# Scratch rows regrouped: fewer, larger DMAs for the attention stacks and the maxima

## The chip, the cores and the metric

The kernel runs on one core of a Trainium2 chip. The metric is the device time of one execution in microseconds (us). The engines that the text names are TensorE (PE in the profile, PEld for its weight loads), VectorE (DVE), ScalarE (ACT), GpSimd (POOL) and SyncE (SP), which here issues every DMA of the kernel.

## The reference

One block of a transformer on 16 batches of 256 tokens of 512 numbers. First a cross attention: 32 heads of 16 numbers, keys and values from a context of 256 tokens of 256 numbers, rotary positions on q and k, and a gated residual. Then a feed-forward part with a squared ReLU (512 to 2048 and back), an expert product weighted by the sum of the two largest routing logits, a layer norm and a second gated residual.

```python
q = apply_axial_rope((layernorm(x) @ Wq).reshape(b, n, 32, 16), pos)
k = apply_axial_rope(k, pos)            # k, v = split(ctx @ Wkv)
w = softmax(einsum('bqhd,bkhd->bhqk', q, k) / 4)
x = x + tanh(g_xattn) * (attn @ Wout + bout)
x = x + tanh(g_ffn) * (layernorm(shared(h) + moe(h)) * gamma + beta)   # h = layernorm(x)
```

## The kernel before

Every float32 product is made of three passes on TensorE: each operand is split into a rounded high part and a rest (`qT[0]`, `qT[1]` and so on, index 0 the high part), and the passes are high x high, rest x high, high x rest.

The program has an attention phase, one batch after the other, and a feed-forward phase. In the attention phase an iteration `i` has 16 steps; at each step TensorE makes the logits of two heads of two batches (`logits_a` for batch `i + 1`, three steps late, and `logits_b` for batch `i`), and the table `SCHEDULE` spreads the other jobs over the steps: turning q and k (`kT1` at step 9, `qT1` at step 12), the projections, the output product. `logits_a` is made only to find the maximum of each row: VectorE's `maxima` reduces it to `mneg`. `logits_b` is the transposed product, with the negative maxima as two further rows, and ScalarE takes its exponential.

A logit needs the contraction over 16 numbers of a head in three passes. They are made in one matmul: the operands are stacked in 48 partitions. In `st_q` the stack is (high, rest, high), in `st_k` (high, high, rest); two heads lie at partitions 0 and 64. The 16 slots of a stack are the 16 steps. Rows 48 and 49 of `st_q` hold the maxima (high part and rest), those of `st_k` ones.

The turned q and k lie in SBUF as 128 partitions, `(l q d)`, of 4 slots of 256 tokens: 4 groups of slots `l`, 2 heads `q`, 16 numbers `d`. `store_turned` writes both parts to a scratch tensor in DRAM (two DMAs of 512 KB, 128 rows of 4 KB). `load_stack` reads from it half a stack (8 slots): for each of the three places in the stack and each of the two heads one DMA of 16 rows and two pieces of 4 KB a row. `load_max` writes the maxima of 8 slots, turned by TensorE to `mT` (16 partitions of 256), into single partitions of `st_q`: for each part and each head one DMA of 8 rows of 1 KB.

SP issues all of this in one written order. An iteration of SP: second half of the stacks of batch `i + 1` (k, then q); x and residual tiles; maxima of the second half of batch `i`; more x and the context; store of k of batch `i + 2`; x1; first half of the k stack of `i + 2`; maxima of the first half of `i + 1`; store of q and first half of the q stack of `i + 2`; x1. A load waits for the store's semaphore before it is issued. TensorE waits for both stacks of a half before steps 3 and 11 (`st_in`) and for the maxima before `logits_b` of steps 0 and 8 (`m_in`).

Of the kernel before, what the change touches and what calls it, by code (L numbers as in the profile page):

```python
# [26 lines left out]
P = 128  # L27
# [20 lines left out]
INC = 16  # L48

Q_PARTS = (0, 1, 0)
K_PARTS = (0, 0, 1)
ROWS_A = 3 * HD
ROWS_B = ROWS_A + 2
STACK_DMAS = 2 * len(Q_PARTS) * 2
PASSES = ((0, 0), (1, 0), (0, 1))


# [83 lines left out]
def flamingo_gated(nc, x, ctxT, posT, g_x, g_f, wq, wkv, wout, bout, gate, up, down, wexp, gamma, beta, out):  # L143
# [1 line left out]
    out_d = out.rearrange("b (t p) d -> (b t) p d", p=P)  # L145
    ctx_d = ctxT.rearrange("b (c p) s -> b p c s", p=P)

    qk_d = [[nc.dram_tensor(f"{x}T_scratch{par}", [2, P, KC * S], F32, kind="Internal").ap() for x in "qk"]
            for par in range(2)]
    x1_d = nc.dram_tensor("x1_scratch", [NT, P, D], F32, kind="Internal").ap()  # L150

    with ExitStack() as stack:
# [67 lines left out]
        aT = [sb1(f"aT{i}", [P, KC, P], F32R) for i in range(2)]  # L220
        xres = [sb1(f"xres{i}", [P, D]) for i in range(2)]
        gbout = sb1("gbout", [P, D])
        mneg = [sb1(f"mneg{i}", [P, TT, NH]) for i in range(2)]
        mT = [sb1(f"mT{i}", [NH // 2, S], F32R) for i in range(2)]
        rot_q1 = sb1("rot_q1", [P, D])
        rot = {"Q0": rot_q0, "Q1": rot_q1, "K0": rot_k, "K1": rot_k}
# [197 lines left out]
        def _(sp):  # L424
# [13 lines left out]
            def store_turned(b, par, x):  # L438

                if some(b - 1):  # L440
                    for half in range(2):
                        sp.wait_ge(st_in[half], INC * STACK_DMAS * (b - 1))
                        alone(sp)
                dst, src = (qk_d[par][0], qT) if x == "q" else (qk_d[par][1], kT)
                sp.wait_ge(taken[BANK[x + "T1"]], number(x + "T1", b))
                alone(sp)
                for part in range(2):
                    sp.dma_start(dst[part], src[part][:].rearrange("p c s -> p (c s)").bitcast(F32)
                                 ).then_inc(turned_out[x], INC)

            def load_stack(b, par, half, x):
                if some((b - 2) * STEPS + 8 * (half + 1)):
                    sp.wait_ge(b_done, (b - 2) * STEPS + 8 * (half + 1))
                    alone(sp)
                slots = slice(8 * half, 8 * half + 8)
                dst, src, parts = ((st_q[par], qk_d[par][0], Q_PARTS) if x == "q" else
                                   (st_k[par], qk_d[par][1], K_PARTS))
                sp.wait_ge(turned_out[x], 2 * INC * (b + 1))
                alone(sp)
                for r, part in enumerate(parts):  # L460
                    heads = src[part].rearrange("(l q d) n -> q d l n", q=2, d=HD)
                    for q in range(2):
                        row = 64 * q + HD * r
                        sp.dma_start(dst[row:row + HD, slots, :].rearrange("d (l c) s -> d l (c s)", c=KC).bitcast(F32),  # L464
                                     heads[q, :, 2 * half:2 * half + 2, :]).then_inc(st_in[half], INC)

            def load_max(b, par, half):
                sp.wait_ge(taken[BANK[f"m{half}"]], number(f"m{half}", b))
                for part in range(2):
                    for q in range(2):  # L470
                        row = 64 * q + ROWS_A + part
                        sp.dma_start(st_q[par][row:row + 1, 8 * half:8 * half + 8, :].bitcast(F32),
                                     mT[part][q:NH // 2:2, :].bitcast(F32)).then_inc(m_in, INC)

            def store_x1(b, t):
                sp.wait_ge(taken[BANK[f"O{t}"]], number(f"O{t}", b))
# [241 lines left out]
        def _(act):  # L718
# [18 lines left out]
            def job(name, i, par):  # L737
                if not live(name, i) or (name not in TWO_STEP and name[0] != "V"):
                    return
                b, par, t = i + LAG[name], (par + LAG[name]) % 2, int(name[-1])  # L740
                bank = BANK[name]
                act.wait_ge(done[bank], number(name, b))
                psum = {"P": pP, "M": pM, "T": pT}[bank]
                turned_psum = psum[:, :].rearrange("p (c s) -> p c s", c=KC)
                cut = slice(t * P, (t + 1) * P)
                if name[0] == "V":
                    if some(b - 1):
                        act.wait_ge(av_done, GROUPS * (b - 1))
                    nc.scalar.copy(v_s[par][:, t, :, 0:HD],
                                   psum[:, :].rearrange("p (h e) -> p h e", h=NH)).then_inc(taken[bank], 1)  # L750
                elif name[0] == "m":
                    if some(2 * b + t):
                        act.wait_ge(m_in, 4 * INC * (2 * b + t))
                    nc.scalar.copy(mT[0][:], psum[0:NH // 2, 0:S]).then_inc(hi_made[bank], 1)
                elif name[0] == "X":
                    nc.scalar.copy(xnT[0][:], turned_psum).then_inc(hi_made[bank], 1)
                elif name[0] == "a":
                    nc.scalar.copy(aT[0][:], turned_psum).then_inc(hi_made[bank], 1)
                else:
                    if some(b):  # L760
                        act.wait_ge(turned_out[name[0]], 2 * INC * b)
                    if name[0] == "q":
                        nc.scalar.mul(qT[0][:, :, cut], turned_psum, SCALE).then_inc(hi_made[bank], 1)
                    else:
                        nc.scalar.copy(kT[0][:, :, cut], turned_psum).then_inc(hi_made[bank], 1)
# [96 lines left out]
        def _(pe):  # L862
# [21 lines left out]
            def job(name, i, par):  # L884
# [11 lines left out]
                if name[0] == "X":  # L896
                    pe.wait_ge(xn_made, TT * b + t + 1)
                    last = turn(psum, lambda c: xn[:, c * P:(c + 1) * P])
                elif name[0] == "Q":
                    last = product(psum[:, :], lambda a, c: xnT[a][:, c, :], lambda w, c: wq_s[w][:, c, :], KC, half)  # L900
                elif name[0] == "K":
                    pe.wait_ge(ctx_split, 2 * b + 2)
                    last = product(psum[:, :], lambda a, c: ctx_s[par][a][:, c, t * P:(t + 1) * P],
                                   lambda w, c: wk_s[w][:, c, :], CC, half)
                elif name[0] == "V":
                    last = product(psum[:, :], lambda a, c: ctx_s[par][a][:, c, t * P:(t + 1) * P],
                                   lambda w, c: wv_s[w][:, c, :], CC, half)
                elif name[0] == "O":
                    last = product(psum[:, :], lambda a, c: aT[a][:, c, :], lambda w, c: wo_s[w][:, c, :], KC, half)
                elif name[0] in "qk":  # L910
                    rope = name[0].upper() + name[-1]
                    pe.wait_ge(roped, len(ROPES) * b + ROPES.index(rope) + 1)
                    last = turn(psum, lambda c: rot[rope][:, c * P:(c + 1) * P])
                elif name[0] == "m":
                    pe.wait_ge(max_done, STEPS * b + 8 * (t + 1))
                    for u in range(TT):
                        last = nc.tensor.transpose(psum[0:NH // 2, u * P:(u + 1) * P],
                                                   mneg[par][:, u, t * 16:(t + 1) * 16], ident[:])
                elif name[:2] == "aT":
                    last = turn(psum, lambda c: attn[t][:, c * P:(c + 1) * P])  # L920
                else:
                    u = int(name[1])
                    pe.wait_ge(av_taken, GROUPS * b + GROUPS // 2 * (t + 1))
                    last = turn(psum, lambda c: av_s[:, GROUPS // 2 * t + c, u * P:(u + 1) * P])
# [14 lines left out]

            def logits_b(b, par, s):  # L940
                if s % 8 == 0:
                    pe.wait_ge(m_in, 4 * INC * (2 * b + s // 8 + 1))
                if some(STEPS * b + s):
                    pe.wait_ge(exp_done, STEPS * b + s)
                for t in range(TT):
                    for q in range(2):
                        rows = slice(64 * q, 64 * q + ROWS_B)
                        last = nc.tensor.matmul(pB[:, q, t * S:(t + 1) * S], st_k[par][rows, s, t * P:(t + 1) * P],  # L948
                                                st_q[par][rows, s, :], start=True, stop=True)
                last.then_inc(b_done, 1)  # L950
# [125 lines left out]
        def _(dve):  # L1076
# [159 lines left out]
            def maxima(b, par, u):  # L1236
                dve.wait_ge(a_done, STEPS * b + u + 1)
                nc.vector.tensor_reduce(  # L1238
                    mneg[par][:, :, 2 * u:2 * u + 2].rearrange("p t q -> p q t"),
                    pA[:, :, :].rearrange("p q (t k) -> p q t k", t=TT), AX.X, ALU.max,  # L1240
                    negate=True).then_inc(max_done, 1)

# [140 lines left out]
```

## Time and profile before

| | us |
|---|---|
| Median of 3 runs | 1703.81 |
| Lowest, highest | 1700.79, 1704.51 |
| The profiled execution | 1698.25 |
| Its span, first to last instruction | 1696.5 |
| PE busy in the span | 1580.5 (93%) |
| PEld busy | 1169.4 (69%) |
| DVE busy | 985.1 (58%) |
| ACT busy | 640.4 (38%) |
| POOL busy | 291.1 (17%) |

The mean granted clock of TensorE is 0.97 of full speed. The DMA queue of SP moved 152.93 MB, and its packets took 38.2% of the time of the 16 DMA engines over the span. "Busy" is the time in which an engine worked on at least one instruction; matmuls are pipelined, so a busy PE need not be at its peak. In the rows, L464 is the DMA of `load_stack`, L472 that of `load_max`, L448 that of `store_turned`, L478 that of `store_x1`, L936 the product of `logits_a`, L948 that of `logits_b`. A window's DMA share is the time that the packets starting in it took, over the 16 engines' time, so it can come out a little over 1; GB/s is what these packets moved.

### The profile page before, as it was taken

How to read it: one execution, taken by the hardware profiler on the slowest of the kernel's cores; microseconds unless marked ns; L12 is line 12 of the kernel's file. 1: busy time of each engine (PE TensorE's matmuls, PEld its weight loads, DVE VectorE, ACT ScalarE, POOL GpSimd, SP SyncE). 2: the span in 40 equal slices, each digit the busy share in tenths (PEclk: the TensorE clock that was granted, in tenths of full speed). 3: DMA queues.
4: the chain of work that ended last, by engine and by line, in shares of the span. 5: the costliest groups of instructions: out<-in, count | busy, mean ns of one | idle time of the engine just before them, and what ended most of it. 6: DMA issues, size and time to landing. Idle time of an engine off the chain costs nothing.

```text
span 1696.5 us, 27932 instructions
## 1 busy us (share of the span) xinstructions
PE 1580.5 (93%) x9760; PEld 1169.4 (69%) x9760; DVE 985.1 (58%) x1460; ACT 640.4 (38%) x960; POOL 291.1 (17%) x363
## 2 busy tenths in 40 slices
PE   3588999999999999988799999999999999999997
PEld 2355666666666666655477788887888878888786
DVE  4577787777778777865455443543435444263524
ACT  2135555555555555555343222221222222222221
POOL 3112222222222222101100110201102010020202
PEclk9679999999999999999799999999999999999999
DMA  3667666666777678773243010100101001010001
GB/s 118 143 145 157 171 141 157 155 147 159 161 144 161 136 158 169 150 144 84 69 124 94 23 35 19 50 26 26 32 19 50 25 26 37 13 50 25 32 19 38
DMA packets 76221, 153.99 MB, mean 91 GB/s; under 512 B 13296, under 2 KB 26608, under 8 KB 76144
## 3 DMA queue, kind: packets, MB, share of 16 engines
q1 hardware_dynamic: 76144, 152.93, 38.2%
q8 instruction: 53, 0.87, 0.2%
q14 instruction: 24, 0.20, 0.0%
HBM read 101.50 MB, written 50.33 MB: 89 GB/s over the span
## 4 chain that ended last, share of the span: by engine, by line
PE 72%; DMA 9%; DVE 8%; SPq 4%; issue 4%; ACT 1%; POOL 1%; DVEq 0%; POOLq 0%; ACTq 0%
PE pP L874 15%; PE pA L1033 10%; PE pO L874 10%; PE pB L1033 10%; PE pT L874 9%; PE pA L936 4%; PE pO L960 4%; DMA stq<-mT 3%; PE pM L874 3%; SPq L464 2%; DVE mneg L1238 2%; PE pB L948 2%; DMA qT_scratch<-qT 2%; PE pM L881 1%; DMA kT_scratch<-kT 1%
## 5 line engine op out<-in xcount | busy, mean ns | idle before, releaser
L1238 DVE TENSOR_REDUCE mneg<-pA 128x4 f32<-128x1024 f32 x256 | 313.1, 1223 | 170.9 <-PE pA L936 168.7
L797 ACT ACTIVATE probs<-pB 128x1024 f32<-128x1024 f32 x256 | 262.5, 1026 | 282.1 <-PE pB L948 274.4
L1308 DVE TENSOR_TENSOR relu<-relu 128x512 f32<-128x512 f32 x128 | 88.3, 690 | 266.6 <-ACT hid L832 266.6
L639 POOL TENSOR_SCALAR var_eps<-meanvar 128x1 f32<-128x1 f32 x96 | 34.5, 360 | 1093.0 <-DVE meanvar L1134 1093.0
L1033 PE MATMUL pA<-dn,hid 128*128 128x512 f32 x768 | 199.0, 394 | 2.8 <-DVE hid L1310 2.1
L1033 PE MATMUL pB<-dn,hid 128*128 128x512 f32 x768 | 196.1, 391 | 0.0
L874 PE MATMUL pO<-fT,up 128*128 128x512 f32 x768 | 188.9, 395 | 3.4 <-issue 3.4
L874 PE MATMUL pP<-fT,up 128*128 128x512 f32 x768 | 190.0, 396 | 0.0
L874 PEld LDWEIGHTS pO<-fT,up 128*128 128x128 f32 x768 | 145.2, 189 | 36.3 <-issue 4.2
L1033 PEld LDWEIGHTS pA<-dn,hid 128*128 128x128 f32 x768 | 142.9, 188 | 38.4 <-DVE hid L1310 7.1
L1033 PEld LDWEIGHTS pB<-dn,hid 128*128 128x128 f32 x768 | 144.2, 188 | 31.0
L936 PE MATMUL pA<-stk,stq 48*128 48x256 f32 x1024 | 133.3, 340 | 33.7 <-DVE mneg L1238 20.4
L874 PEld LDWEIGHTS pP<-fT,up 128*128 128x128 f32 x768 | 142.4, 188 | 30.9
L936 PEld LDWEIGHTS pA<-stk,stq 48*128 48x128 f32 x1024 | 79.5, 192 | 107.2 <-issue 63.5
L960 PE MATMUL pO<-probs,v 128*17 128x256 f32 x2048 | 140.2, 393 | 0.6 <-ACT probs L797 0.6
L825 ACT ACTIVATE relu<-pO 128x512 f32<-128x512 f32 x64 | 38.3, 599 | 254.8 <-PE pO L874 246.3
L948 PE MATMUL pB<-stq,stk 50*128 50x256 f32 x1024 | 106.8, 286 | 11.2 <-DMA stq<-mT 8.8
L825 ACT ACTIVATE relu<-pP 128x512 f32<-128x512 f32 x64 | 38.3, 599 | 197.9 <-PE pP L874 197.9
L874 PE MATMUL pP<-wq,xnT 128*128 128x512 f32 x384 | 108.7, 421 | 1.6 <-DVE xnT L1154 1.6
L874 PE MATMUL pT<-wo,aT 128*128 128x512 f32 x384 | 106.7, 423 | 2.8 <-DVE aT L1180 2.8
L874 PEld LDWEIGHTS pP<-wq,xnT 128*128 128x128 f32 x384 | 73.2, 200 | 29.7 <-issue 12.9
L874 PE MATMUL pT<-ex,fT 128*128 128x512 f32 x384 | 93.6, 392 | 0.0
(131 smaller groups left out, 1963.6 us busy)
## 6 DMA issues: line engine op xcount, KB each, us to landing
stk<-kT_scratch SPq DMA_DIRECT2D x192, 128.0 KB, 5.3
stq<-qT_scratch SPq DMA_DIRECT2D x192, 128.0 KB, 5.7
kT_scratch<-kT SPq DMA_DIRECT2D x32, 512.0 KB, 3.1
qT_scratch<-qT SPq DMA_DIRECT2D x32, 512.0 KB, 3.5
xin<-x SPq DMA_DIRECT2D x32, 256.0 KB, 7.3
xres<-x SPq DMA_DIRECT2D x32, 256.0 KB, 9.6
x_scratch<-xres SPq DMA_DIRECT2D x32, 256.0 KB, 3.7
fx<-x_scratch SPq DMA_DIRECT2D x32, 256.0 KB, 2.7
```

The source lines that it names most:

```text
L464: sp.dma_start(dst[row:row + HD, slots, :].rearrange("d (l c) s -> d l (c s)", c=KC).bitcast(F32), heads[q, :, 2 * half:2 * half + 2, :]). ...
L639: nc.gpsimd.tensor_scalar_add(var_eps[:], meanvar[:, 1:2], EPS).then_inc(ve_made, 1)
L797: nc.scalar.activation(probs[:, s % 4, :, :, :].rearrange("p a b s -> p a (b s)"), pB[:, :, :], ACT.Exp).then_inc(exp_done, 1)
L825: nc.scalar.activation(relu[m % 2][:], pU[m % 2], ACT.Relu).then_inc(relu_made, 1)
L874: last = nc.tensor.matmul(dst, lhs(a, c), rhs(w, c), start=(c == 0 and (a, w) == PASSES[0]), stop=(c == chunks_ - 1 and (a, w) == PASSES[-1]))
L881: last = nc.tensor.transpose(dst[:, c * P:(c + 1) * P], src(c), ident[:])
L936: last = nc.tensor.matmul(pA[:, q, t * S:(t + 1) * S], st_q[par][rows, s, t * P:(t + 1) * P], st_k[par][rows, s, :], start=True, stop=True)
L948: last = nc.tensor.matmul(pB[:, q, t * S:(t + 1) * S], st_k[par][rows, s, t * P:(t + 1) * P], st_q[par][rows, s, :], start=True, stop=True)
L960: last = nc.tensor.matmul(pO[32 * j:32 * j + HD + 1, 0:S], v_s[par][:, t, 4 * g + j, :], probs[:, (2 * g + j // 2) % 4, j % 2, t, :], star ...
L1033: last = nc.tensor.matmul(acc[u], hid[m % 2][x_][:, u * P:(u + 1) * P], dn_s[w][:, m, :], start=(m == 0 and k == 0), stop=(m == MC - 1 and ...
L1238: nc.vector.tensor_reduce(mneg[par][:, :, 2 * u:2 * u + 2].rearrange("p t q -> p q t"), pA[:, :, :].rearrange("p q (t k) -> p q t k", t=TT ...
L1308: nc.vector.tensor_tensor(r[:], r[:], r[:], ALU.mult).then_inc(sq_made, 1)
```

## The change

The scratch tensor of q and k is laid out as 2 parts of 32 rows (2 heads of 16 numbers) of all 16 slots, so that a row of a stack is one piece of 8 KB per half. The store writes the same 4 KB pieces to other places: its destination is `l r m`, 4 groups by 32 rows by 1024 numbers. `load_stack` takes two neighbouring places of the stack at once where their parts are 0 and 1 (q: places 0 and 1, then 2; k: place 0, then 1 and 2): four DMAs, two of 256 KB and two of 128 KB, not six of 128 KB. The columns of `mneg` are ordered by head and then slot, so that `mT` holds the 8 slots of one head and then those of the other, and `load_max` writes both heads' rows, partitions 48 and 112 or 49 and 113, with one DMA of 16 KB. The counts that wait for these DMAs follow.

```diff
--- before.py
+++ after.py
@@ -49,11 +49,11 @@
 
 
 
-Q_PARTS = (0, 1, 0)
-K_PARTS = (0, 0, 1)
+Q_RUNS = ((0, 0, 2), (2, 0, 1))
+K_RUNS = ((0, 0, 1), (1, 0, 2))
 ROWS_A = 3 * HD
 ROWS_B = ROWS_A + 2
-STACK_DMAS = 2 * len(Q_PARTS) * 2
+STACK_DMAS = 2 * len(Q_RUNS) * 2
 PASSES = ((0, 0), (1, 0), (0, 1))
 
 
@@ -145,7 +145,7 @@
     out_d = out.rearrange("b (t p) d -> (b t) p d", p=P)
     ctx_d = ctxT.rearrange("b (c p) s -> b p c s", p=P)
 
-    qk_d = [[nc.dram_tensor(f"{x}T_scratch{par}", [2, P, KC * S], F32, kind="Internal").ap() for x in "qk"]
+    qk_d = [[nc.dram_tensor(f"{x}T_scratch{par}", [2, 2 * HD, STEPS * S], F32, kind="Internal").ap() for x in "qk"]
             for par in range(2)]
     x1_d = nc.dram_tensor("x1_scratch", [NT, P, D], F32, kind="Internal").ap()
 
@@ -220,7 +220,7 @@
         aT = [sb1(f"aT{i}", [P, KC, P], F32R) for i in range(2)]
         xres = [sb1(f"xres{i}", [P, D]) for i in range(2)]
         gbout = sb1("gbout", [P, D])
-        mneg = [sb1(f"mneg{i}", [P, TT, NH]) for i in range(2)]
+        mneg = [sb1(f"mneg{i}", [P, TT, 2, 2, NH // 4]) for i in range(2)]
         mT = [sb1(f"mT{i}", [NH // 2, S], F32R) for i in range(2)]
         rot_q1 = sb1("rot_q1", [P, D])
         rot = {"Q0": rot_q0, "Q1": rot_q1, "K0": rot_k, "K1": rot_k}
@@ -445,7 +445,8 @@
                 sp.wait_ge(taken[BANK[x + "T1"]], number(x + "T1", b))
                 alone(sp)
                 for part in range(2):
-                    sp.dma_start(dst[part], src[part][:].rearrange("p c s -> p (c s)").bitcast(F32)
+                    sp.dma_start(dst[part].rearrange("r (l m) -> l r m", l=STEPS // KC),
+                                 src[part][:].rearrange("p c s -> p (c s)").bitcast(F32)
                                  ).then_inc(turned_out[x], INC)
 
             def load_stack(b, par, half, x):
@@ -453,24 +454,23 @@
                     sp.wait_ge(b_done, (b - 2) * STEPS + 8 * (half + 1))
                     alone(sp)
                 slots = slice(8 * half, 8 * half + 8)
-                dst, src, parts = ((st_q[par], qk_d[par][0], Q_PARTS) if x == "q" else
-                                   (st_k[par], qk_d[par][1], K_PARTS))
+                dst, src, runs = ((st_q[par], qk_d[par][0], Q_RUNS) if x == "q" else
+                                   (st_k[par], qk_d[par][1], K_RUNS))
                 sp.wait_ge(turned_out[x], 2 * INC * (b + 1))
                 alone(sp)
-                for r, part in enumerate(parts):
-                    heads = src[part].rearrange("(l q d) n -> q d l n", q=2, d=HD)
+                for r, part, n in runs:
                     for q in range(2):
                         row = 64 * q + HD * r
-                        sp.dma_start(dst[row:row + HD, slots, :].rearrange("d (l c) s -> d l (c s)", c=KC).bitcast(F32),
-                                     heads[q, :, 2 * half:2 * half + 2, :]).then_inc(st_in[half], INC)
+                        sp.dma_start(dst[row:row + n * HD, slots, :].rearrange("d l s -> d (l s)").bitcast(F32),
+                                     src[part:part + n, HD * q:HD * (q + 1), 8 * half * S:8 * (half + 1) * S]
+                                     ).then_inc(st_in[half], INC)
 
             def load_max(b, par, half):
                 sp.wait_ge(taken[BANK[f"m{half}"]], number(f"m{half}", b))
                 for part in range(2):
-                    for q in range(2):
-                        row = 64 * q + ROWS_A + part
-                        sp.dma_start(st_q[par][row:row + 1, 8 * half:8 * half + 8, :].bitcast(F32),
-                                     mT[part][q:NH // 2:2, :].bitcast(F32)).then_inc(m_in, INC)
+                    row = ROWS_A + part
+                    sp.dma_start(st_q[par][row:row + 65:64, 8 * half:8 * half + 8, :].bitcast(F32),
+                                 mT[part][:].bitcast(F32)).then_inc(m_in, INC)
 
             def store_x1(b, t):
                 sp.wait_ge(taken[BANK[f"O{t}"]], number(f"O{t}", b))
@@ -750,7 +750,7 @@
                                    psum[:, :].rearrange("p (h e) -> p h e", h=NH)).then_inc(taken[bank], 1)
                 elif name[0] == "m":
                     if some(2 * b + t):
-                        act.wait_ge(m_in, 4 * INC * (2 * b + t))
+                        act.wait_ge(m_in, 2 * INC * (2 * b + t))
                     nc.scalar.copy(mT[0][:], psum[0:NH // 2, 0:S]).then_inc(hi_made[bank], 1)
                 elif name[0] == "X":
                     nc.scalar.copy(xnT[0][:], turned_psum).then_inc(hi_made[bank], 1)
@@ -915,7 +915,7 @@
                     pe.wait_ge(max_done, STEPS * b + 8 * (t + 1))
                     for u in range(TT):
                         last = nc.tensor.transpose(psum[0:NH // 2, u * P:(u + 1) * P],
-                                                   mneg[par][:, u, t * 16:(t + 1) * 16], ident[:])
+                                                   mneg[par][:, u, t, :, :].rearrange("p q l -> p (q l)"), ident[:])
                 elif name[:2] == "aT":
                     last = turn(psum, lambda c: attn[t][:, c * P:(c + 1) * P])
                 else:
@@ -939,7 +939,7 @@
 
             def logits_b(b, par, s):
                 if s % 8 == 0:
-                    pe.wait_ge(m_in, 4 * INC * (2 * b + s // 8 + 1))
+                    pe.wait_ge(m_in, 2 * INC * (2 * b + s // 8 + 1))
                 if some(STEPS * b + s):
                     pe.wait_ge(exp_done, STEPS * b + s)
                 for t in range(TT):
@@ -1236,7 +1236,7 @@
             def maxima(b, par, u):
                 dve.wait_ge(a_done, STEPS * b + u + 1)
                 nc.vector.tensor_reduce(
-                    mneg[par][:, :, 2 * u:2 * u + 2].rearrange("p t q -> p q t"),
+                    mneg[par][:, :, u // 8, :, u % 8].rearrange("p t q -> p q t"),
                     pA[:, :, :].rearrange("p q (t k) -> p q t k", t=TT), AX.X, ALU.max,
                     negate=True).then_inc(max_done, 1)
```

## Rows read from the trace of the kernel before

**Rows 1.** Page, 40 slices of the span: busy tenths of DMA.

```profile
DMA  3667666666777678773243010100101001010001
```

**Rows 2.** Busy time by stage: window, then us (instructions) of each engine, clock, DMA.

```profile
40.00:85.00 45.00, 23.70 (x89) 16.03 (x88) 25.40 (x36) 8.23 (x15) 8.50 (x10) 0.70 0.65 135
...
410.00:455.00 45.00, 43.99 (x382) 29.74 (x380) 35.72 (x50) 25.41 (x36) 11.24 (x12) 1.00 0.73 159
...
845.00:1160.00 315.00, 311.29 (x1377) 250.89 (x1376) 144.66 (x234) 91.03 (x151) 30.34 (x49) 0.99 0.17 51
```

**Rows 3.** SP's queue, first and last k store: start us, length, what.

```profile
41.68 0.81 SPq L448 DMA_DIRECT2D kT_scratch<-kT  x2
...
730.03 0.81 SPq L448 DMA_DIRECT2D kT_scratch<-kT  x2
```

**Rows 4.** Chain of waits, 320 to 560 us: start, length, what.

```profile
481.70 6.91 DMA stq<-mT
488.73 0.51 PE pB L948 x4
```

**Rows 5.** Waits: who <- for what: us in total, times, longest.

```profile
PE pA L936 <- DMA stq<-qT_scratch: 12.5, 5, 7.5
...
PE pB L948 <- DMA stq<-mT: 8.8, 9, 1.8
...
PEld pB L948 <- DMA stq<-mT: 6.5, 7, 1.6
```

**Rows 6.** Lines 464 and 472: shortest/median/longest ns of issuing one DMA.

```profile
L464 SPq DMA_DIRECT2D stk<-kT_scratch x192: 302/423/1767, 45.7 to 751.0; - x192
...
L472 SPq DMA_DIRECT2D stq<-mT x128: 634/635/1096, 94.9 to 800.5; - x128
```

**Rows 7.** SP's queue, one steady batch and a lone set of maxima.

```profile
417.82 0.82 SPq L448 DMA_DIRECT2D qT_scratch<-qT  x2
...
438.09 0.40 SPq L436 DMA_DIRECT2D ctx_raw<-ctxT  x1
452.64 0.81 SPq L448 DMA_DIRECT2D kT_scratch<-kT  x2
...
456.74 2.67 SPq L464 DMA_DIRECT2D stk<-kT_scratch  x6
...
462.86 0.83 SPq L448 DMA_DIRECT2D qT_scratch<-qT  x2
...
782.60 2.67 SPq L472 DMA_DIRECT2D stq<-mT  x4
```

**Rows 8.** DMA traffic, 782.5 to 786.6 us, then 41.5 to 45.65 us.

```profile
DMA  0000000000000300000030000021000003000300
...
DMA packets 65, 0.04 MB, mean 10 GB/s; under 512 B 32, under 2 KB 64, under 8 KB 64
...
q1 hardware_dynamic: 64, 0.03, 3.8%
...
DMA packets 288, 1.05 MB, mean 253 GB/s; under 512 B 32, under 2 KB 32, under 8 KB 288
...
kT_scratch<-kT SPq DMA_DIRECT2D x2, 512.0 KB, 3.1
```

**Rows 9.** Busy time by stage, four stretches with much DMA traffic.

```profile
46.50:50.00 3.50, 1.77 (x6) 1.33 (x7) 2.70 (x3) 3.21 (x7) 2.50 (x4) 0.50 0.98 167
408.60:411.00 2.40, 2.40 (x21) 1.74 (x23) 1.57 (x3) 1.70 (x4) 0.00 (x0) 1.00 1.02 408
...
2.50:8.00 5.50, 0.00 (x0) 0.00 (x0) 0.00 (x0) 2.52 (x3) 5.50 (x2) 1.00 0.96 296
8.00:12.00 4.00, 0.00 (x0) 0.00 (x0) 3.71 (x9) 0.00 (x0) 2.33 (x4) 1.00 0.80 289
```

**Rows 10.** TensorE's timeline: steps 3 and 8 of the batch in rows 7.

```profile
429.97 0.50 PE L936 MATMUL pA<-stk,stq 48*128 48x256 f32 x4
...
443.13 0.50 PE L948 MATMUL pB<-stq,stk 50*128 50x256 f32 x4
```


## The prediction

> **What bounds the kernel now.** I read the slices of the page first, then busy time by stage, then the chain of waits through one batch, then the queue of SyncE (SP), and last the DMA traffic of chosen microseconds. The slices show two phases: the DMA digits stand at 6 to 7 in the first half and fall to 0 to 3 in the second [rows 1]. The stages say the same of TensorE: in a steady 45 us stretch of the attention phase it works 43.99 us, and from 845 us on, in the feed-forward phase, nearly all the time [rows 2]. So the attention phase is bound by TensorE, one batch each 45.9 us on average: the 16 stores of k issue from 41.68 to 730.03 us, 688.35 us for 15 intervals [rows 3]. The feed-forward phase holds none of the changed DMAs; what the change does, it does before about 800 us.
>
> The transfers are not far below TensorE, though: the 16 DMA engines are busy 0.73 of that steady stretch [rows 2], and in some batches TensorE waits for the maxima's rows. In the chain, the transfer `stq<-mT` runs 6.91 us from 481.70, and the `pB` product of step 8 starts at 488.73 [rows 4]. Over the run these waits are small: 8.8 us of the matmul row and 6.5 us of the weight-load row [rows 5].
>
> **The change part by part.** Per batch it takes away 8 of 24 stack DMAs and 4 of 8 maxima DMAs, at 423 and 635 ns of issuing each [rows 6]: 8 x 0.42 + 4 x 0.635 = 5.9 us of SP's time. SP has it to spare (it waits between 438 and 452 us, for k's second turned half [rows 7]), so by itself it is worth nothing but where SP stands on the chain, in the waits of [rows 5]. The maxima's new column order costs nothing: VectorE writes four numbers per step either way, and the transpose reads 16 adjacent columns either way. No wait is added; only the counts of two are halved or reduced by a third.
>
> What decides is the shape of each new DMA. The trace shows how a shape meets the engines. In 4.1 us in which only four maxima DMAs run [rows 7], each of 8 rows, there are 32 packets of data and 32 under 512 B: 8 small ones for each DMA. Two stores of 128 rows leave 256 packets of data and 32 small ones, 16 each [rows 8]. A DMA thus closes with one small packet per engine that it ran on; 128 rows gave 16 engines, 8 rows gave 8. The split goes by the outermost rows.
>
> Now the outermost counts after the edit. The part with two pieces reads `src[0:2, 16 rows, 2048]`: its source has an outermost count of 2, since the 16 rows wanted of each piece are not adjacent to the next piece's. The single part has 16, as before. The store writes `l r m` with l = 4 against 128 partitions: outermost 4. The maxima write 2 partitions from 16: outermost 2. By the row on 8, I take 2 engines, 16, 4 and 2. The bounds are 16 engines for all (rival B) and these counts; I take these because the 8-row DMAs are the only row of a short outermost side.
>
> The Trainium skill, page "DMA: Bandwidth & Descriptors", section "Why a DMA increments its semaphore by 16 and not by 1", states this as a rule: the engines are the largest number up to 16 that divides the outermost counts of both sides, and they are the lowest-numbered ones. The trace agrees with the first half (8 for 8 rows); no row here shows which engines. By it the sum below holds; by the opposite, rival B.
>
> Which engines is an unknown of its own. Ends: always the same two or four, so that all these DMAs queue behind each other, or others each time (rival C). I take the same, since all of them go through one queue, which has no reason to turn.
>
> The speed of one engine: in stores, 408 GB/s at a share of 1.02 is 408 / 16 / 1.02 = 25.0 GB/s. Loads of 128 rows give 289 / 16 / 0.80 = 22.6 and 296 / 16 / 0.96 = 19.3, and the present stack loads, 16 engines into 16 partitions, 167 / 16 / 0.98 = 10.6 [rows 9]. For two engines that write 16 partitions each I take 25.0: their sum of 50 GB/s is far below the 167 that the same rows took. 10.6 stays as the other end.
>
> So one engine's share is 256 KB / 2 = 131,072 B, 5.24 us, for a two-piece part, and 512 KB / 4 = 131,072 B, 5.24 us, for a store. Engine 0's work per batch:
> - Stores: 4 x 5.24 = 21.0.
> - Stacks, 4 half stacks of 2 x 5.24 + 2 x 0.33 (8 KB each): 4 x 11.14 = 44.6.
> - Seven whole tiles (x, the residual, x1, two each, and the context), 16 KB of each on an engine: 7 x 0.66 = 4.6.
> - Maxima: the four DMAs of [rows 8] took 3.8% of 16 engines for 4.1 us, 2.49 us, or 0.078 per data packet with its small one; 32 data packets per batch now lie on engine 0, some 2.2 us (an estimate).
>
> Together 72.4 us, against 45.9 for a whole batch now: engine 0 becomes the bound. It also stands idle where the chain leaves it:
> - From the maxima of the second half landing to the k store: step 8's product at 443.13 to the issue at 452.64 [rows 7, 10] is 9.5, about 1.2 more to the first packet (issue at 782.60, first traffic in the fourteenth of 40 slices of 782.5 to 786.6 [rows 7, 8]), less 1.3 for the x and context tiles that run in it: 9.4.
> - Each turn from a store to its load: 456.74 - 452.64 = 4.10 from issue to issue [rows 7], less 1 MB at 408 GB/s, 2.57: 1.5, twice.
>
> That makes 12.4 and a period of 72.4 + 12.4 = 84.8. The order on the ring is forced: q's load of half 0, the other half of k and q, tiles, maxima of the second half, gap, store of k, load, maxima, store of q, load. TensorE cannot pass step 3 before q's load is in, nor step 8 before the maxima that queue behind three half stacks; the five steps between (13.2 us, 429.97 to 443.13 [rows 10]) lie beside those loads. The q store is ready in time: it issues 10.2 us after the k store now [rows 7], and engine 0 is then busy for 22 us.
>
> The clock: where TensorE worked 23.70 of 45 us, the granted clock was 0.70 [rows 2]; at 44 of 85 us I expect like stretches at the lower of its two levels, and gap one grows by about 2 us: 87.
>
> The sum, against the execution profiled (1,698.3, span 1,696.5): 15 intervals x (87 - 45.9) = 616; less 10 for the first, which has no second-half maxima to wait for; plus 40 for the last batch, whose store, load and second half are as long but have no next store after them: 646. So 2,344, and as the median of the runs shown is 5.6 above that execution, 2,350.
>
> **The rivals.**
> - **B, faster.** If a two-piece part goes over 16 engines (its 32 rows counted as one), the change does what it says. Place: the maxima's rows at step 8, issued behind the stack loads. They would come at least 2 x 0.635 us sooner, plus the shorter issuing ahead of them. It decides from the point at which those waits vanish, and can give no more than all the waits of [rows 5], 15.3 us for the maxima and 12.5 for the stack loads (matmul row); about 20: 1,698 - 20 + 5.6 = 1,684. For it: the bytes are the same and the pieces longer. The Trainium skill, same page, section "Rules for kernel authors", advises coalescing small transfers, those under 64 KB being mostly overhead. The trace shows 8 KB DMAs at 635 ns of issue each, but the rule leaves out what 8 rows show. Against it: the 8 small packets per DMA.
> - **B', no change:** as B, with all of it hidden behind TensorE: 1,704.
> - **C, few engines but others each time.** No queueing; each transfer is alone 5.24 us long. From the q store's issue at 417.82 to step 3's first product at 429.97 there are 12.15 us [rows 7, 10]; store and load would take two times 1.2 + 5.24 + 0.3, and 0.6 of issuing, 14.1: 2 us late each batch, 32 in all: 1,735.
> - **D, only some are narrow.** Loads alone on two engines: the stores' 10.5 fall to 2.6, twice, the period to 71: 2,090. Stores alone on four: the q chain is 10.5 - 2.6 = 7.9 longer with some 2.5 of slack, +5.4 each batch: 1,790.
> - **A with slow reads:** at 19.3 GB/s the eight two-piece parts take 12.4 us longer per batch, 2,545; at 10.6, 57 longer, about 3,250.
>
> **How the numbers follow.** Chances: A 0.80 (its own range 2,200 to 2,600), D 0.09, B 0.06, C 0.03, B' 0.02. The range of eight in ten takes A but for its slowest end and D's narrow loads: 2,050 to 2,650. A measurement of this kernel can tell 0.2% (3.4 us) from no change; faster by that is B alone, 0.06; the same is B', 0.02; slower is the rest, 0.92.
>
> **What would show it.** Right: in steady stretches of the attention phase the mean DMA share falls to about 0.2 and the rate to 80 to 90 GB/s, though DMA is the bound (two engines full, twelve nearly idle); TensorE works about 44 to 50 of 87 us with a granted clock under 0.9; k stores come some 87 us apart; the stores take 10 us or more to land against 3, two-piece loads 10 or more; the maxima leave 2 small packets per DMA; the chain lies on DMA for most of the attention phase. The feed-forward phase is as long as before. Wrong: a share still near 0.7 with 16 small packets per stack DMA (B); long landings with a period under 50 (C); k stores landing in 3 us (D). If the count is right and the size is not, the speed of an engine that reads 8 KB pieces is the term to look at.

## The result: 2,455.6 us, 1.44 times the time before

The changed kernel takes 2455.58 us (median of 4 runs, 2449.66 to 2459.01), the kernel before 1704.16 us beside it: a ratio of 1.4391, 95% interval 1.4324 to 1.4458. The prediction was 2,350 us in a range of 2,050 to 2,650.

The page of the changed kernel, slices of the span and totals of the DMA queue:

```profile
span 2457.2 us, 27740 instructions
...
PE   3234546456456455455455464799999999999998
...
PEclk8557778678677777777777786999999999999999
DMA  3222222222222212222222212331101001010010
...
DMA packets 64572, 153.96 MB, mean 63 GB/s; under 512 B 7792, under 2 KB 21104, under 8 KB 58352
```

On this page DMA looks idle: digits of 2 through the attention phase where [rows 1] has 6 and 7, while the phase now fills 25 of 40 slices. The count of packets under 512 B, one for each engine that a DMA ran on, comes out exactly: 128 two-piece loads x 2, 128 single ones x 16, 64 stores x 4, 64 maxima x 2, 263 other DMAs x 16 and 896 small pieces of data (routing weights, positions, the two gates) make 256 + 2,048 + 256 + 128 + 4,208 + 896 = 7,792.

One batch of it and a stretch of the feed-forward phase by busy time (window, length, busy us and instructions of PE, PEld, DVE, ACT, POOL, clock, DMA share, GB/s), against [rows 2]:

```profile
596.70:690.45 93.75, 50.72 (x382) 33.43 (x382) 35.63 (x51) 25.37 (x37) 11.12 (x12) 0.76 0.24 76
...
1605.70:1920.70 315.00, 310.44 (x1373) 250.18 (x1373) 144.73 (x234) 90.20 (x150) 30.56 (x49) 0.99 0.16 51
```

TensorE works 50.72 of 93.75 us at a granted clock of 0.76, and DMA shows a share of 0.24. The second window lies as far from the end as 845 to 1160 us did before, and PE's 310.44 us in it stand beside the 311.29 of [rows 2]: the feed-forward phase is untouched.

SP's queue, first and last store of k and one batch, against [rows 3, 7]:

```profile
41.06 1.31 SPq L448 DMA_DIRECT2D kT_scratch<-kT  x2
...
501.24 1.20 SPq L448 DMA_DIRECT2D kT_scratch<-kT  x2
...
516.46 2.20 SPq L464 DMA_DIRECT2D stk<-kT_scratch  x4
...
520.30 1.16 SPq L448 DMA_DIRECT2D qT_scratch<-qT  x2
541.02 2.25 SPq L464 DMA_DIRECT2D stq<-qT_scratch  x4
...
544.72 2.10 SPq L464 DMA_DIRECT2D stk<-kT_scratch  x4
547.02 9.66 SPq L464 DMA_DIRECT2D stq<-qT_scratch  x4
...
564.39 3.38 SPq L472 DMA_DIRECT2D stq<-mT  x2
...
568.64 6.42 SPq L436 DMA_DIRECT2D ctx_raw<-ctxT  x1
596.70 1.20 SPq L448 DMA_DIRECT2D kT_scratch<-kT  x2
...
1447.38 1.16 SPq L448 DMA_DIRECT2D kT_scratch<-kT  x2
```

The 15 intervals are 1,406.3 / 15 = 93.75 us long (45.9 before). The sum closes: 15 x (93.75 - 45.89) = 718, plus 1,009.8 - 966.5 = 43 more from the last k store to the end, less 0.6 before the first, is the 760.7 by which the spans differ.

The chain of waits through that batch, against [rows 4]:

```profile
501.89 14.48 DMA kT_scratch<-kT
...
520.91 20.03 DMA qT_scratch<-qT
...
542.85 14.77 DMA stq<-qT_scratch
...
557.75 0.80 PE pA L936 x4
...
565.66 18.46 DMA stq<-mT
...
584.24 0.79 PE pB L948 x4
```

Four transfers, 14.48 + 20.03 + 14.77 + 18.46 = 67.7 of 95.5 us. Over the span TensorE's waits in [rows 5] have grown so:

```profile
PE pB L948 <- DMA stq<-mT: 393.6, 30, 18.6
PEld pB L948 <- DMA stq<-mT: 332.0, 24, 18.8
PE pA L936 <- DMA stq<-qT_scratch: 292.5, 16, 44.2
```

And this is what two engines look like. Both stretches lie in the loads of three half stacks that SP issues from 541.02 on:

```profile
543.40:546.90 3.50, 0.00 (x0) 0.00 (x0) 0.00 (x0) 0.00 (x0) 1.02 (x1) 0.92 0.95 222
549.00:554.50 5.50, 0.00 (x0) 0.00 (x0) 0.00 (x0) 0.00 (x0) 0.00 (x0) 0.50 0.13 54
```

From 549 to 554.5 us every compute engine stands still, and the DMA share is 0.13, 2.1 of 16 engines, at 54 GB/s: 54 / 16 / 0.13 = 26 GB/s each. The packets before that show that these are the same two all along. From 542.4 to 549.0 us the trace has 70 packets under 512 B, which is 14 engines times the five DMAs that use all 16 (two single parts of q, the x1 tile, two single parts of k), and 112 packets of 2 KB, which is 14 engines times 8 of the tile. So 14 engines were through with all five while two still had the two-piece parts of q ahead of them.

### The profile page after: what moved, and what is told of

Read it like the earlier page. It is cut to its first block, busy times and chain, and to the rows that moved or that the text cites. A ratio compares the mean times of both kernels' runs of the same rounds, so it can differ in the third digit from the quotient of the medians.

```text
span 2457.2 us, 27740 instructions
## 1 busy us (share of the span) xinstructions
PE 1677.0 (68%) x9760; PEld 1224.2 (50%) x9760; DVE 984.5 (40%) x1460; ACT 638.6 (26%) x960; POOL 289.5 (12%) x363
## 2 busy tenths in 40 slices
DMA packets 64572, 153.96 MB, mean 63 GB/s; under 512 B 7792, under 2 KB 21104, under 8 KB 58352
## 4 chain that ended last, share of the span: by engine, by line
DMA 45%; PE 43%; SPq 4%; DVE 4%; issue 3%; ACT 1%; POOL 0%; DVEq 0%; POOLq 0%; ACTq 0%
DMA qT_scratch<-qT 13%; DMA stq<-mT 11%; PE pP L874 10%; DMA stq<-qT_scratch 10%; DMA kT_scratch<-kT 9%; PE pA L1033 7%; PE pO L874 7%; PE pB L1033 7%; PE pT L874 5%; SPq L464 2%; PE pA L936 2%; PE pO L960 1%; DMA stk<-kT_scratch 1%; PE pB L948 1%; PE pM L881 1%
## 5 line engine op out<-in xcount | busy, mean ns | idle before, releaser
L948 PE MATMUL pB<-stq,stk 50*128 50x256 f32 x1024 | 122.9, 322 | 396.7 <-DMA stq<-mT 393.6
L936 PE MATMUL pA<-stk,stq 48*128 48x256 f32 x1024 | 143.1, 361 | 313.5 <-DMA stq<-qT_scratch 292.5
L948 PEld LDWEIGHTS pB<-stq,stk 50*128 50x128 f32 x1024 | 93.3, 220 | 406.2 <-DMA stq<-mT 332.0
L936 PEld LDWEIGHTS pA<-stk,stq 48*128 48x128 f32 x1024 | 86.6, 209 | 393.1 <-issue 263.0
L960 PE MATMUL pO<-probs,v 128*17 128x256 f32 x2048 | 163.5, 445 | 0.6 <-ACT probs L797 0.6
L874 PE MATMUL pP<-wq,xnT 128*128 128x512 f32 x384 | 140.2, 516 | 1.6 <-DVE xnT L1154 1.6
L874 PEld LDWEIGHTS pP<-wq,xnT 128*128 128x128 f32 x384 | 92.9, 254 | 40.9 <-issue 17.8
L669 POOL TENSOR_TENSOR xres<-xres,gbout 128x512 f32<-128x512 f32 x32 | 40.1, 1273 | 607.5 <-DMA xres<-x 607.5
```

The costliest lines, as they stand in the source:

```text
L669: nc.gpsimd.tensor_tensor(xres[t][:], xres[t][:], gbout[:], ALU.add).then_inc(res_made, 1)
L874: last = nc.tensor.matmul(dst, lhs(a, c), rhs(w, c), start=(c == 0 and (a, w) == PASSES[0]), stop=(c == chunks_ - 1 and (a, w) == PASSES[-1]))
L936: last = nc.tensor.matmul(pA[:, q, t * S:(t + 1) * S], st_q[par][rows, s, t * P:(t + 1) * P], st_k[par][rows, s, :], start=True, stop=True)
L960: last = nc.tensor.matmul(pO[32 * j:32 * j + HD + 1, 0:S], v_s[par][:, t, 4 * g + j, :], probs[:, (2 * g + j // 2) % 4, j % 2, t, :], star ...
```

## Experiments

In all of them "16 engines" means that a DMA leaves 16 small packets, and "wide" and "narrow" mean many engines and few. The edits are shortened to the lines that matter: `...` stands for code left out, and the counts of those who wait for these DMAs follow each time.

**Loads alone wide** (`load16`).

```diff
-for r, part, n in runs:
+for r, part, n in [(r + k, part + k, 1) for r, part, n in runs for k in range(n)]:
```

> The changed kernel, but each two-piece load is issued as two DMAs of 16 rows of 8 KB (six per half stack again); layout, store and maxima stay as changed. Theory (engine count: outermost 2 puts a load on two engines, outermost 4 a store on four, always the same ones): only the stores and maxima stay narrow, a stack DMA closes with 16 small packets, 1,780 to 1,900 us. Rival (the layout, pieces of 8 KB at a pitch of 16 KB, or the larger DMAs' length): the layout is the same, so still over 2,300 us.

Measured 2011.74 us, ratio 1.1812 (1.1744 to 1.1881). The layout theory falls: the same layout is 444 us faster. The engine count's figure was too low, for its chain is longer than that sum had it. SP's queue in this kernel:

```profile
501.89 1.21 SPq L448 DMA_DIRECT2D kT_scratch<-kT  x2
...
516.88 2.65 SPq L464 DMA_DIRECT2D stk<-kT_scratch  x6
...
521.18 1.16 SPq L448 DMA_DIRECT2D qT_scratch<-qT  x2
534.96 2.63 SPq L464 DMA_DIRECT2D stq<-qT_scratch  x6
...
567.02 1.20 SPq L448 DMA_DIRECT2D kT_scratch<-kT  x2
```

The store of k takes 15.0 us to its load, and only then may SP go on to q's store: 19.3 us after k's, where it was 10.2 [rows 7]. Then 13.8 for q's store, and 32.1 to the next k store. The sum had only q's own store.

**Stores alone wide** (`store16`).

```diff
-sp.dma_start(dst[part].rearrange("r (l m) -> l r m", l=4), src[part][...])
+for g in range(4):
+    sp.dma_start(dst[part, :, g * 1024:(g + 1) * 1024], src[part][32 * g:32 * (g + 1)][...])
```

> The changed kernel, but each store is issued as four DMAs of 32 rows, one per group of slots (eight per store of both parts); loads and maxima stay as changed. Theory: stores on 16 engines again, k's store to load 4 to 6 us in place of 15.2, and engine 0 relieved of 16 us a batch: 2,090 to 2,200 us. Rival (layout): no change, 2,455 us.

Measured 2182.57 us, ratio 1.2804 (1.273 to 1.2877): the theory's range. Its page counts 11632 small packets, as 16 for each of its store DMAs and 2 for each two-piece load make it.

**All wide in the changed layout** (`all16`): both edits, and the maxima as four DMAs of 8 rows.

> The changed kernel's scratch layout and order of maxima columns, with every DMA split so that 16 (stack loads, stores) or 8 (maxima) rows are outermost: 24 stack loads, 16 store DMAs and 8 maxima DMAs a batch. Theory: back to the kernel before within 1.5%, 1,690 to 1,730 us, DMA share about 0.7. Rival (layout): over 2,300 us.

Measured 1760.83 us, ratio 1.0334 (1.0281 to 1.0387), some 30 us above the theory's range and far from the rival's. So 695 of the 751 us were the count of engines; the rest lies in the layout or the DMAs that it needs. Periods, from the k stores of each trace: 50.0 here, 65.7 with narrow stores and maxima, 76.7 with narrow loads and maxima, 93.75 with all narrow. 15.7 and 26.7 add up to 42.4 of the 43.8: the costs are in series.

**The maxima alone** (`max2`), on the kernel before: the change's `load_max`, `mneg` and counts, nothing else.

> The kernel before with the change's maxima alone: one DMA of 16 KB for both heads' rows, outermost 2, two of them per half. Theory: two engines for it, 2 small packets each, but a few KB on engines that no other narrow DMA fills: 1,695 to 1,712 us, at most the lost waits for the maxima gained. Rival (it is the maxima on two engines that cost, since they stand on the chain for 11% of the changed kernel's span): over 1,750 us.

Measured 1701.98 us, ratio 0.9996 (0.9961 to 1.0031). Two engines for 16 KB cost nothing that this comparison can tell (0.4%) while no other narrow DMA fills them.

**The same two engines, or others each time?** (`split_slots`)

```diff
+for h in range(n):
+    low, w = 8 * half + 4 * h, 8 // n
+    sp.dma_start(dst[row:row + n * HD, low:low + w, :]..., src[part:part + n, ..., low * S:(low + w) * S])...
```

> The changed kernel with each two-piece load cut in two DMAs of four slots each (outermost still 2, same bytes, twice as many DMAs of half the length). Theory (always the same two engines, so that only their sum of bytes counts): no change but the issuing, 2,440 to 2,490 us. Rival (each DMA is alone on two engines of its own, and its length is what counts): the loads take half as long, 2,150 to 2,300 us.

Measured 2462.82 us, ratio 1.4494 (1.4418 to 1.4569), with 8048 small packets, 256 more for 128 more DMAs. Halving the length of each transfer helps nothing; their sum counts. Rival C falls.

**The pitch** (`pad_after`, `pad_all16`): a scratch row of 20 KB.

```diff
-qk_d = [[nc.dram_tensor(..., [2, 2 * HD, STEPS * S], ...).ap() ...
+qk_d = [[nc.dram_tensor(..., [2, 2 * HD, STEPS * S + 1024], ...).ap()[:, :, 0:STEPS * S] ...
```

> The changed kernel with a scratch row 4 KB longer (pitch 20 KB, not 16 KB); counts of engines unchanged. Theory of the missing 6.8 us per batch: at a pitch of 16 KB the four engines of a store meet in the same places of DRAM, hence 293 ns per 4 KB in its first microseconds and 159 later; with the new pitch a store takes 12 us, not 15.2: 2,350 to 2,410 us. Rival (the slow start has another cause): 2,440 to 2,470 us.

> The kernel of all16 (every DMA on 16 or 8 engines, the changed layout) with the pitch of 20 KB. If the pitch slows its stack loads and stores: under 1,740 us. If not: 1,750 to 1,772 us, as all16.

With `pad_after` 2443.59 us, ratio 1.4382 (1.4307 to 1.4457): no difference to the changed kernel. The slow start of its stores is still there (from 1.2 to 4.2 us after the issue 69 / 16 / 0.32 = 13.5 GB/s an engine, 74 / 16 / 0.34 = 13.6 in the changed kernel), so it has another cause. With `pad_all16` 1734.54 us, ratio 1.0212 (1.0162 to 1.0263) against 1.0334 (1.0281 to 1.0387) of `all16`: a small gain, the two intervals just apart, where loads and stores run on 16 engines.

**What `all16` loses** (`before_stores8`): the kernel before with each store in eight DMAs.

```diff
-sp.dma_start(dst[part], src[part][...])
+for g in range(4):
+    sp.dma_start(dst[part, 32 * g:32 * (g + 1)], src[part][32 * g:32 * (g + 1)][...])
```

> The kernel before with its stores alone cut in four DMAs of 32 rows per part (eight per store), as in all16. If the six more issues on SP ahead of each load are what all16 loses: 1,735 to 1,765 us. Rival (the 8 KB pieces of its stack loads lose it): 1,700 to 1,712 us.

Measured 1745.98 us, ratio 1.0277 (1.023 to 1.0324): most of `all16`'s loss is its stores. The two kernels lose it in the same place: TensorE's matmul row waits 52.3 us for q's stack here and 47.8 in `all16`, 12.5 before [rows 5]. SP's queue of `all16`, and the traffic of its store (window, engines, clock, share, GB/s):

```profile
543.32 3.59 SPq L450 DMA_DIRECT2D kT_scratch<-kT  x8
...
548.82 2.62 SPq L466 DMA_DIRECT2D stk<-kT_scratch  x6
...
544.40:546.80 2.40, 2.40 (x20) 1.64 (x22) 1.55 (x3) 1.68 (x4) 0.00 (x0) 1.00 0.98 265
```

Eight issues take 3.59 us for 0.81 before, and k's store to its load is 5.50 us for 4.10. The issuing alone could make that: 3.59, 0.3 for the last 128 KB at 408 GB/s and the 1.5 of a turn are 5.4 us (an estimate). But the packets are slower too: 265 GB/s at a share of 0.98, 16.9 an engine, where the store of 128 rows had 408 and 25.0 [rows 9]. `before_stores8`, with the old scratch order, shows the same (263 GB/s at 0.98 from 540.2 to 542.6 us). So here stores that read 32 partitions a DMA ran slower than those that read 128; how much of their 47 and 57 us is the issuing and how much the rate, these two kernels do not tell. The Trainium skill, page "SBUF — State Buffer", section "Door 1: The DMA port swizzle", has the rule: the rate of a DMA goes by how many of 16 ports its partitions reach. The trace agrees in direction (0.65 of the rate); by that section's table 32 partitions in a row reach 8 ports, half of them, and no run here shows the ports.

**Larger DMAs that stay wide** (`inter`, `inter_dup`): the two parts of a number as neighbouring rows, in DRAM and in the stack.

```diff
+# scratch [2 * HD, 2, STEPS * S + 1024]: head and number, part, slots
+sp.dma_start(dst[row:row + 32], src[16 * q:16 * q + 16, :, cols].rearrange("d w n -> (d w) n"))  # q: 32 rows
+# k's repeated part: two DMAs into every other row (inter), or one with a repeated source (inter_dup)
+for g in range(4):   # a store of both parts
+    sp.dma_start(dst[:, :, g * 1024:(g + 1) * 1024], qTa[32 * g:32 * (g + 1)])
```

> A layout in which the larger DMAs of the change stay on 16 engines: the scratch row order is head, number, part (pitch 20 KB a part), the two parts of a number are neighbouring rows of the stack (order of the contraction is free), so q's two places are one DMA of 32 rows, all outermost; k's repeated part goes into every other row by two DMAs of 16; a store is four DMAs of 32 rows that hold both parts; maxima as changed. A batch has 32 of these DMAs where the kernel before has 36 and the changed one 24. Theory (the count of engines is all that was wrong with the change): within 1% of the kernel before, 1,685 to 1,715 us. Rival (8 KB pieces or a store in more DMAs lose by themselves): over 1,725 us.

> The same, with k's repeated part read by one DMA whose source repeats each row (outermost 16 against 32 rows): four DMAs per half stack, as in the change, 28 a batch. Theory: 16 small packets for it, 1,680 to 1,712 us. Rival: that DMA falls to fewer engines or the pieces lose by themselves, over 1,725 us.

Measured 1751.9 us, ratio 1.0333 (1.0301 to 1.0366), and 1721.74 us, 1.0157 (1.0126 to 1.0187). `inter` came out in the rival's range, `inter_dup` lies between the two. Both have 16 engines for every store and stack load (12,400 and 11,376 small packets in all, which is 16 for each; the maxima stay on 2) and fewer DMAs than `all16`, and both still lose: in `inter_dup` k's store at 521.99 has its load at 529.36, 7.4 us for 4.10 before. Here the issuing does not explain it: four issues take 3.24 us, and with 0.6 for the last 256 KB and 1.5 of a turn they would make 5.4 us (an estimate). The packets ran at 228 GB/s with a share of 0.99 from 523.2 to 527.2 us, 14.4 an engine. Nor do the more numerous small packets: 48 of 271 in that window, 79 of 234 in that of `all16`.

**Stores of 128 rows, larger loads** (`inter_old`): neighbouring parts, but in the old scratch order.

```diff
-qk_d: [2, P, KC * S]
+qk_d: [P, 2, KC * S]
-for part in range(2): sp.dma_start(dst[part], src[part]...)         # before: two of 512 KB per store
+sp.dma_start(dst.rearrange("p w n -> p (w n)"), qTa[...])            # one, 128 rows of 8 KB
+rows = src.rearrange("(l r) w n -> r w l n", r=32)
+sp.dma_start(dst[row:row + 32], rows[16 * q:16 * q + 16, :, 2 * half:2 * half + 2, :])   # q: 32 rows
+for w in range(2):                                                   # k: every other row
+    sp.dma_start(dst[row + w:row + 32:2], rows[16 * q:16 * q + 16, 0, 2 * half:2 * half + 2, :])
```

> The scratch of the kernel before, 128 rows of groups, heads and numbers, with the two parts of a row side by side: a store is one DMA of 128 rows of 8 KB (16 engines), q's two neighbouring places are one DMA of 32 rows with two pieces of 4 KB (32 outermost, 16 engines, twice as many partitions as before), k's repeated part goes into every other row by two DMAs; maxima as changed. 26 of these DMAs a batch, 36 before, and none of the stores of 32 rows that cost all16, inter and inter_dup 1.4 to 3.3 us each. Theory (what those kernels lose is the turn from store to load): at or below the kernel before, 1,680 to 1,705 us. Rival (fewer, larger DMAs lose by themselves even on 16 engines): over 1,715 us.

Measured 1676.12 us, ratio 0.9892 (0.9864 to 0.992): 1.1% below the kernel before, with an interval clear of 1. Its waits for stack data, all that the trace has, and its first and last k store:

```profile
PEld pA L947 <- DMA stq<-qT_scratch: 9.0, 3, 6.8
...
PE pA L947 <- DMA stq<-qT_scratch: 7.8, 3, 6.1
...
40.83 0.33 SPq L449 DMA_DIRECT2D kT_scratch<-kTa  x1
...
715.51 0.33 SPq L449 DMA_DIRECT2D kT_scratch<-kTa  x1
```

The waits for the maxima's rows of [rows 5] have fallen from 8.8 and 6.5 us to 2.1 and 0.9, those of the matmul row for q's stack from 12.5 to 7.8, and the period is 674.7 / 15 = 44.98 us. Between the first and the last k store 13.7 us are gone; the two matmul rows fell by 11.4.

## Why the prediction was right, and by how much it was off

- **TensorE bounds the attention phase with DMA not far below:** right; see `inter_old`, whose trace has 3.0 us left of the 15.3 of the maxima's waits in [rows 5] and which gains 18.7 us, where rival B put about 20. Which of its parts gives how much was not taken apart.
- **The engines go by the outermost rows, 2 and 4:** shown, by 7,792 packets and by the three kernels that undo it.
- **The same engines each time:** shown by the stretch with a share of 0.13, by the 14 engines that ran ahead before it, and by `split_slots`. Which two of the 16 they are, no run shows.
- **25.0 GB/s for an engine, the slow end left out:** right where an engine is alone (26), not all the time; see below.
- **The period, 87:** it was 93.75 on average. The batch shown is 95.5 long, and its steps, against the forecast's terms (each tile put where SP issues it): k's store to its load 15.2, 12.7 forecast; from there to q's load 24.6, 24.2; to step 3 16.7, 12.3; to step 8 26.5, 26.0; to the next k store 12.5, 11.5. Of the 8.8 us, two steps hold 6.9.
- **Mis-sized, q's load (4.4 us):** from 543.4 to 546.9 us all engines are busy (0.95) at 222 GB/s, 14.6 each: the single parts of q and k and the x1 tile run on the other 14, and the two that matter are slow meanwhile. From 542.4 to 549.0 us there are 78 packets of 8 KB; 14 x 4 = 56 are the single parts', which leaves 22 for the two, 22 x 8 KB / 6.6 us / 2 = 13.7 GB/s each, half of the 26 that they had alone. At 25.0 their 11 packets each would have taken 3.6 us, so this stretch holds some 3 of the 4.4. The prediction had priced the single parts at 0.33 us on engine 0 and put nothing for what they do to others. That it is the traffic of the 14 that slows the two is argued from these numbers; no run took it away.
- **Mis-sized, k's store (2.5 us):** the four engines start at half their speed. The store in `load16`, first and then later:

```profile
502.40:505.40 3.00, 2.90 (x28) 2.13 (x29) 2.16 (x4) 2.23 (x4) 0.00 (x0) 1.00 0.19 45
509.00:513.00 4.00, 4.00 (x35) 2.55 (x34) 2.47 (x4) 1.39 (x2) 0.00 (x0) 1.00 0.25 99
```

45 / 16 / 0.19 = 14.8 GB/s each at first, 99 / 16 / 0.25 = 24.8 later. The pitch is not it (`pad_after`). The same section of the Trainium skill (page "SBUF — State Buffer") puts partitions 32 apart on one port. If the four engines walk from partitions 0, 32, 64 and 96 in step, which no trace here shows, two would share a port and might have half the speed until they drift apart: a guess. No run here takes that apart, so the cause stays open.
- **Tail and start:** the last batch cost 43 us more (40 forecast), the first interval was 82.5 us, 11 less than the mean (10 forecast).
- **The clock:** under 0.9, as put: 0.76 granted where TensorE works 50.72 of 93.75 us. Gap one, from step 8 to the k store, is 12.5 us where 11.5 was put.
- **The other signs:** a DMA share of 0.24 and 76 GB/s, where about 0.2 and 80 to 90 were put; the longer period lowers the rate.
- **D, which did not come:** "stores alone on four: 1,790" was wrong, 2,012 measured: the chain was followed from q's store alone, and SP's order puts k's store, its landing and its load ahead of it. "Loads alone: 2,090" was 2,183; that kernel's split stores may be some 57 us of it, for `all16`, which has them too, lost as much against the kernel before.

## What to carry to other kernels

Before merging DMAs, write down the outermost count of both sides of each new one. In these runs it set how many engines carried it (2, 4 and 8 for such counts, 16 for 16, 32 and 128), and DMAs with few ran one after the other on the same ones, however idle the mean DMA share looked. Fewer, larger DMAs paid here only where stacks and stores kept counts that gave 16 engines and a store read all 128 partitions: that layout, with neighbouring parts, is 1.1% faster than the kernel before, where the change as made was 44% slower. In a queue written out in one order, a transfer that gets longer delays all that is issued behind the wait for it, so its chain starts at the first of them.

## What the runs showed of the hardware that was not expected

- SP itself is held up while two engines have much queued. The four loads of a half stack issue in 2.25 us at 541.02, those at 547.02, the third half stack in a row, take 9.66, and the context tile at 568.64 takes 6.42 (the queue above). Where only the loads are narrow (`store16`) the third half stack takes 9.55 at 519.86; where only they are wide (`load16`) its six take 2.62 at 541.82 and the context tile 0.40.
- Stores of 32 partitions a DMA moved 265 GB/s (`all16`), 263 (`before_stores8`) and 228 (`inter_dup`), one of 128 moved 408, all in pieces of 4 KB and on 16 engines.
- A pitch 4 KB longer made `all16` 1.2% faster and left the narrow kernel as it was. Why was not tried.
